# Splitting the near and the state products of a state space layer into runs, with the near products two blocks ahead

## The chip, the cores and the metric

The kernel runs on one core of a Trainium2 chip, as one program with one launch. The metric is the device time of one execution in microseconds (us), as the median over several executions. TensorE (PE) multiplies, VectorE (DVE), ScalarE (ACT) and GpSimd (POOL) do the rest, SyncE (SP) starts most of the transfers. PSUM, the memory that PE writes to, has 8 banks; a bank holds 512 numbers of 32 bits in each of 128 partitions.

## What is computed

A chain of layers on one sequence of 2048 rows with 128 channels: a mixture of experts, attention in a window, the experts again, a latent attention with its experts, **a state space layer**, and the latent attention with its experts once more. The change concerns the state space layer alone:

```python
def _L1_attn_ref(u, A_log, D, C_re, C_im, log_dt):
    dt = jnp.exp(log_dt)
    A = -jnp.exp(A_log)
    t = jnp.arange(L_, dtype=u.dtype)
    at = dt[:, None, None] * A[None, None, :] * t[None, :, None]
    K = jnp.einsum('mn,mln->ml', C_re, jnp.exp(at))
    u_f = jnp.fft.rfft(u.transpose(0, 2, 1), n=2 * L_)
    k_f = jnp.fft.rfft(K, n=2 * L_)
    y = jnp.fft.irfft(u_f * k_f, n=2 * L_)[..., :L_]
    return y.transpose(0, 2, 1) + u * D
...
x = x + _L1_attn_ref(_layernorm(x, axis=-1), ...)
```

Each channel is convolved with a kernel of its own that is a sum of 64 decaying exponentials, and gets its input times `D` and the residual added.

## The kernel before

Each layer is a stage. `leave_stage()` stands between stages: PE, DVE, ACT and POOL raise one semaphore when they are through, and all five engines wait for all four. So nothing of the following stage starts before the last instruction of the state space stage has ended.

`state_space` cuts the 2048 rows into `NT` = 16 tiles of 128 rows. For a channel m, what a tile gets from its own rows is a product with a 128x128 Toeplitz matrix (`toep[:, m, :]`); what it gets from all former tiles comes through 64 states. The steps:

1. `layer_norm` on DVE makes `Y`, tile by tile.
2. The states' inputs (L1999): 128 products, one for each channel, weights `b_in` 128x64, moving operand 16 columns of `Y`. They fill PSUM banks 0 and 1.
3. DVE copies these banks out (L2028), and one scan (L2030) runs the recurrence over the 16 tiles. `r_scanned` says that it is done.
4. DVE blanks banks 0 to 3 (L2032, four memsets), each raising `r_cleared`. The products write only 16 of every 32 partitions of a bank, and ACT reads all of them.
5. Eight blocks k of 16 channels each, block k in bank `k % 4`. A block has four groups (`qd`), and each group four **near** products (L2013: weights `Y[:, :, m]` 128x16, moving `toep` 128x128) and then four **far** or state products (L2020: weights the states 64x16, moving `E_far` 64x128), which add to the same places. The four of a group, q = 0 to 3, write partitions 32q to 32q+15: they lie in four column groups of PE's array. The far products take rows 0 to 63 or 64 to 127 of the array, by the parity of m.
6. After a block, ACT copies its bank into a row buffer in reversed order (L2045, raises `r_rows`), PE turns the four squares back (`turn_back`, L1992, into bank `4 + k % 2`, raises `r_turned`), and DVE adds the result to `X` (L2037, raises `r_added`).

PE's program is the plain order of the code: near and far of block k, `turn_back(k)`, near and far of block k+1. `turn_back(k)` waits for `r_rows` of its own block. POOL makes `Y * D` and adds it to `X` beside step 2 (`r_skip`).

The name `arena` in the profile is a large buffer that holds the inputs, the states and `toep`; `big_w` holds `E_far`; `ACCn` holds the row buffers; `Yn` is `Y`. In the stage before (latent attention) stands a line that the prediction uses, L1688: 16 products with weights 128x32 and a moving operand of 128x128, four after four into the four column groups, as near products do. L1618 uses the four column groups as well, L1592 and L1602 use half of the rows and all columns.

Of the kernel before, what the change touches and what calls it, by code (L numbers as in the profile page):

```python
# [12 lines left out]
P = 128  # L13
T = 2048
NT = T // P
# [33 lines left out]
def bcast(ap, n):  # L49
    return ap.unsqueeze(len(ap.shape)).broadcast_to(list(ap.shape) + [n])  # L50
# [27 lines left out]
def build(nc, ins, out, upto=6):  # L78
    with ExitStack() as ctx:
        pe, dve, act, pool, sp = nc.tensor, nc.vector, nc.scalar, nc.gpsimd, nc.sync  # L80
# [4 lines left out]
        def sem(name):  # L85
            return ctx.enter_context(nc.semaphore(name))


        psum = ctx.enter_context(nc.psum_tensor("psum", [P, 8, GW], F32))

        X, Yn, ACCn = sb("X", [P, NT, D]), sb("Yn", [P, NT, D + 1]), sb("ACCn", [P, NT, D + 1])
        Y, ACC = Yn[:, :, 0:D], ACCn[:, :, 0:D]
# [21 lines left out]
        def take(start, n, dt=F32):  # L114
            part = arena[:, start:start + n]
            return part if dt is F32 else part.bitcast(dt)
# [26 lines left out]
        toep = take(0, D * P).rearrange("p (m x) -> p m x", m=D)  # L143
# [23 lines left out]
        def chain(instruction):  # L167

            instruction.then_inc(dve_step.sem, dve_step.up())
            dve.wait_ge(dve_step.sem, dve_step.n)  # L170

        def leave_stage(pool_beside=None):

            for e in (pe, dve, act, pool):
                e.drain().then_inc(stage_left, 1)
            stages[0] += 1
            if pool_beside is not None:
                pool_beside()
            for e in (pe, dve, act, pool, sp):
                e.wait_ge(stage_left, 4 * stages[0])  # L180
# [29 lines left out]
        def own_pool(instruction):  # L210

            instruction.then_inc(pool_step.sem, pool_step.up())
            pool.wait_ge(pool_step.sem, pool_step.n)
# [55 lines left out]
        def layer_norm(n, x_ready):  # L269
            for g in range(NG + 1):  # L270
                if g:
                    ln_rows(n, g - 1)
                if g < NG:
                    x_ready(g)
                    ln_statistics(n, g)
                    ln_rooted(n, g)
# [459 lines left out]
        def windowed_attention(n, f, x_ready):  # L736
# [404 lines left out]
            for g in range(NG):  # L1141
# [19 lines left out]
        back_in, rates_in, pair_made, rates_made, far_made, far_scaled, taps_out, toep_in, neg_made, near_made, near_exp = (  # L1161
            sem(n) for n in ("back_in", "rates_in", "pair_made", "rates_made", "far_made", "far_scaled", "taps_out", "toep_in",
                             "neg_made", "near_made", "near_exp"))
# [726 lines left out]
        def latent_block(B, n, c, f, x_ready, far):  # L1890
# [76 lines left out]
        r_padded, r_decay, r_skip, r_states_in, r_scanned, r_cleared, r_made, r_rows, r_turned, r_added = (  # L1967
            sem(n) for n in ("r_padded", "r_decay", "r_skip", "r_states_in", "r_scanned", "r_cleared", "r_made", "r_rows", "r_turned", "r_added"))
        C17 = NT + 1

        def state_space(n, x_ready):
            state_in, states, mult = (take(k * K, 64 * C17) for k in (96, 101, 106))
            v3 = lambda t: t.rearrange("p (a c) -> p a c", a=64)
            ysb = [ACC[:, 4 * i:4 * i + 4, :] for i in range(4)]
            layer_norm(n, x_ready)

            def ssm_pool():
                pool.memset(v3(state_in)[:, :, 0:1], 0.0)
                pool.memset(v3(mult)[:, :, 0:1], 0.0).then_inc(r_padded, 1)
                pool.tensor_copy(v3(mult)[:, :, 1:C17], bcast(decay[:], NT)).then_inc(r_decay, 1)  # L1980
                pool.wait_ge(skip_in, 16)
                pool.wait_ge(ln_normed, NT * (n + 1))
                own_pool(pool.tensor_tensor(ACC[:, :, :], Y[:, :, :], skip_d.unsqueeze(1).broadcast_to([P, NT, D]), ALU.mult))
                pool.tensor_tensor(X[:, :, :], X[:, :, :], ACC[:, :, :], ALU.add).then_inc(r_skip, 1)

            def ssm_pe():
                def turn_back(k):
                    pe.wait_ge(r_rows, k + 1)
                    if k >= 2:
                        pe.wait_ge(r_added, k - 1)  # L1990
                    for qd in range(4):
                        mm = pe.transpose(psum[:, 4 + k % 2, qd * P:(qd + 1) * P], ysb[k % 4][:, qd, :], ident[:])  # L1992
                    mm.then_inc(r_turned, 1)

                pe.wait_ge(near_exp, D // STEP)
                pe.wait_ge(ln_normed, NT * (n + 1))
                for a in range(64):
                    for r in range(2):
                        mm = pe.matmul(psum[64 * r:64 * r + 64, a // 32, (a % 32) * NT:(a % 32 + 1) * NT],  # L1999
                                       b_in[:, 2 * a + r, :], Y[:, :, 2 * a + r], start=True, stop=True)  # L2000
                mm.then_inc(r_states_in, 1)
                pe.wait_ge(toep_in, 16 * 8)
                st3 = v3(states)
                for k in range(8):
                    b = k % 4
                    if k < 4:
                        pe.wait_ge(r_cleared, k + 1)
                    else:
                        pe.wait_ge(r_rows, k - 3)
                    for qd in range(4):  # L2010
                        for q in range(4):
                            m = 16 * k + 4 * qd + q
                            pe.matmul(psum[32 * q:32 * q + NT, b, qd * P:(qd + 1) * P], Y[:, :, m], toep[:, m, :], start=True, stop=False,  # L2013
                                      skip_group_check=True)
                        if qd == 0 and k == 0:
                            pe.wait_ge(r_scanned, 1)
                        for q in range(4):
                            m = 16 * k + 4 * qd + q
                            r = 64 * (m % 2)
                            mm = pe.matmul(psum[32 * q:32 * q + NT, b, qd * P:(qd + 1) * P], st3[r:r + 64, m // 2, 0:NT],  # L2020
                                           E_far[r:r + 64, m // 2, 0:P], start=False, stop=True, skip_group_check=True)
                    mm.then_inc(r_made, 1)
                    turn_back(k)

            def ssm_dve():
                dve.wait_ge(r_states_in, 1)
                dve.wait_ge(r_padded, 1)
                chain(dve.tensor_copy(v3(state_in)[:, :, 1:C17], psum[:, 0:2, :].rearrange("p b (a c) -> p (b a) c", c=NT)))  # L2028
                dve.wait_ge(r_decay, 1)
                dve.tensor_tensor_scan(states, mult, state_in, 0.0, ALU.mult, ALU.add).then_inc(r_scanned, 1)  # L2030
                for b in range(4):
                    dve.memset(psum[:, b, :], 0.0).then_inc(r_cleared, 1)  # L2032
                dve.wait_ge(r_skip, 1)
                for k in range(8):
                    dve.wait_ge(r_turned, k + 1)
                    dst = X[:, :, 16 * k:16 * k + 16]
                    dve.tensor_tensor(dst, psum[:, 4 + k % 2, :].rearrange("p (m c) -> p c m", c=32)[:, 0:NT, :], dst, ALU.add).then_inc(r_added, 1)  # L2037

            def ssm_act():
                act.wait_ge(r_skip, 1)  # L2040
                for k in range(8):
                    act.wait_ge(r_made, k + 1)
                    if k >= 4:
                        act.wait_ge(r_turned, k - 3)
                    act.activation(ysb[k % 4], psum[:, k % 4, :].rearrange("p (k x) -> p k x", k=4)[:, :, ::-1], ACT.Copy).then_inc(r_rows, 1)  # L2045

            ssm_pool()
            ssm_pe()
            ssm_dve()
            ssm_act()  # L2050
            leave_stage()
# [84 lines left out]
```

## Time and profile before

| | |
|---|---|
| median of 3 runs | 1747.12 us (1745.82 to 1751.17) |
| the profiled execution | 1757.22 us |
| its span | 1755.9 us |
| mean granted clock of TensorE | 0.834 of 2.4 GHz |
| busy: PE, DVE, ACT, POOL | 1238.1, 1196.7, 947.0, 570.0 us |
| first product of the state space stage to its last add | 1075.17 to 1130.47 us |

A time in a row is counted from the start of the span. "Idle before" an instruction is time in which its engine did nothing, and the name behind the arrow is what ended it. An f32 product stands in the trace as two records on PE (a transpose as one). The granted clock is 1.00 at 2.4 GHz and 0.50 at 1.2 GHz; the chip grants it by what PE did before. The last chain of waits, which ends with the store, says nothing of this stage: it is read from the stretch between its two barriers.

### The profile page before, as it was taken

Reading aid. Unit: us, or ns where it says so; the run is one execution under the profiler, and the core shown is the slowest. Engines: PE = TensorE matmul, PEld = TensorE weight load, DVE = VectorE, ACT = ScalarE, POOL = GpSimd, SP = SyncE. Lnnn points to the kernel's source line nnn. Section 1 sums busy time; section 2 is a strip of 40 time slices with the busy share of each in tenths; the row PEclk is TensorE's granted clock in tenths of the full one; section 3 lists DMA queues with packets and bytes.
Section 4 is the critical chain, followed back from the end, with each engine's and each line's share of the span. In section 5 each row is a group of like instructions: output and inputs, shape, how many; then the busy total and the mean of one; then the engine's idle time right before and its main releaser. Section 6 shows DMA issues by size and latency. Waiting matters only on the chain. (4 is left out here: it accounts for less than half of the span.)

```text
span 1755.9 us, 36353 instructions
## 1 busy us (share of the span) xinstructions
PE 1238.1 (71%) x13313; PEld 624.7 (36%) x13313; DVE 1196.7 (68%) x3279; ACT 947.0 (54%) x1500; POOL 570.0 (32%) x1032
## 2 busy tenths in 40 slices
PE   2754564366757788899886464776778898988746
PEld 2653453365532122222232453353222222223246
DVE  4358598436777899987862354277789999786234
ACT  0226774122445688888875240134557788887522
POOL 2331276146662411321123242275332111112323
PEclk9977675577577999999998695856799999999869
DMA  9410000021001100000000180000000000000012
GB/s 243 102 46 1 1 4 2 22 66 50 1 18 53 35 1 1 1 2 3 1 1 13 49 217 27 2 1 1 1 1 2 1 2 1 1 2 1 13 44 81
DMA packets 59137, 49.01 MB, mean 28 GB/s; under 512 B 7105, under 2 KB 54194, under 8 KB 58610
## 3 DMA queue, kind: packets, MB, share of 16 engines
q1 hardware_dynamic: 53282, 35.84, 7.9%
q0 software_dynamic: 4736, 9.74, 1.7%
q8 instruction: 109, 1.79, 0.4%
q10 hardware_dynamic: 944, 1.10, 0.2%
q14 instruction: 66, 0.54, 0.1%
HBM read 32.72 MB, written 18.38 MB: 29 GB/s over the span
## 5 line engine op out<-in xcount | busy, mean ns | idle before, releaser
L1709 ACT ACTIVATE arena<-psum 128x1024 f32<-128x1024 f32 (+3 forms) x640 | 561.0, 898 | 191.6 <-PE psum L1602 170.8
L1761 DVE TENSOR_REDUCE arena<-psum 128x1 f32<-128x512 f32 x768 | 479.8, 683 | 63.4 <-PE psum L1592 59.7
L1618 PE MATMUL psum<-arena 128*9 128x256 f32 (+2 forms) x4352 | 346.4, 394 | 0.9 <-POOL arena L1826 0.4
L1592 PE MATMUL psum<-arena 64*128 64x512 bf16 (+3 forms) x1280 | 240.2, 371 | 128.7 <-DVE arena L1761 58.3
L1766 DVE CUSTOM_DVE_ANT_0 arena<-psum,wqkv 128x384 bf16<-128x384 f32 (+3 forms) x512 | 230.3, 486 | 89.0 <-PE psum L1592 75.1
L1602 PE MATMUL psum<-arena 64*128 64x512 bf16 (+3 forms) x1280 | 233.7, 362 | 20.0 <-ACT arena L1709 15.0
L1826 POOL TENSOR_SCALAR_AFFINE_SELECT arena<-arena 128x256 f32<-128x256 f32 x256 | 103.6, 408 | 323.0 <-ACT arena L1709 320.4
L1592 PEld LDWEIGHTS psum<-arena 64*128 64x128 bf16 x1280 | 64.0, 94 | 383.2 <-DVE arena L1761 196.6
L1618 PEld LDWEIGHTS psum<-arena 128*9 128x9 f32 x4352 | 67.7, 89 | 174.3 <-issue 133.5
L1804 POOL CAST arena<-arena 128x16 bf16<-128x16 f32 x64 | 16.4, 257 | 327.7 <-DVE arena L1772 325.4
L677 DVE TENSOR_SCALAR small<-psum,YT 128x128 f32<-128x128 f32 x168 | 50.5, 342 | 78.0 <-PE psum L587 77.4
L632 ACT ACTIVATE small<-psum,YT 128x128 f32<-128x128 f32 x168 | 52.4, 364 | 83.5 <-PE psum L587 64.6
L587 PE MATMUL psum<-arena,YT 128*128 128x128 f32 x672 | 97.1, 292 | 0.1
L1602 PEld LDWEIGHTS psum<-arena 64*128 64x128 bf16 x1280 | 63.5, 95 | 93.1 <-ACT arena L1709 46.6
L1714 ACT ACTIVATE arena<-psum 128x1024 bf16<-128x1024 bf16 x64 | 65.5, 1023 | 52.3 <-PE psum L1580 48.3
L587 PEld LDWEIGHTS psum<-arena,YT 128*128 128x128 f32 x672 | 87.6, 204 | 2.9 <-issue 1.3
L578 PE MATMUL psum<-ident,ACCn 128*128 128x128 f32 x16 | 7.2, 470 | 90.7 <-DMA ACCn<-sorted_rows 58.1
L559 POOL DMA_INDIRECT made_rows<-arena,index x38 | 42.4, 1116 | 76.8 <-DVE arena L657 75.1
L545 POOL DMA_INDIRECT sorted_rows<-Yn,slot x32 | 31.4, 980 | 83.9 <-DVE slot L363 74.8
L597 PE MATMUL psum<-w,small 128*128 x304 | 43.0, 286 | 15.7 <-ACT small L632 12.7
L1580 PE MATMUL psum<-identb,arena 128*128 128x128 bf16 x512 | 44.5, 237 | 9.9 <-DVE psum L1750 3.9
L597 PE MATMUL psum<-big_w,small 128*128 x368 | 50.5, 281 | 0.6 <-issue 0.6
(353 smaller groups left out, 1962.9 us busy)
## 6 DMA issues: line engine op xcount, KB each, us to landing
arena<-taps SPq DMA_DIRECT2D x8, 1024.0 KB
big_w<-in_w SPq DMA_DIRECT2D x2, 2048.0 KB
ACCn<-made_rows SPq DMA_DIRECT2D x16, 256.0 KB, 3.6
regions<-sorted_rows SPq DMA_DIRECT2D x5, 741.8 KB, 4.6
sorted_rows<-arena SPq DMA_DIRECT2D x2, 1483.5 KB, 16.8
ACCn<-regions SPq DMA_DIRECT2D x32, 64.5 KB, 1.9
w<-in_w SPq DMA_DIRECT2D x2, 1024.0 KB
ACCn<-sorted_rows SPq DMA_DIRECT2D x6, 258.0 KB, 3.4
```

What stands on the lines that cost most here:

```text
L587: mm = pe.matmul(hidden_of(s, k), first[s % 2][:, k * P:(k + 1) * P], xt[s // GT % 2][:, (s % GT) * P:(s % GT + 1) * P], start=True, stop= ...
L597: mm = pe.matmul(psum[:, 4 + s % 2, 0:D], hid[s % 2][:, k, :], flat2[:, bass.ds(expert[s] * HID + k * P, D)], start=(k == 0), stop=(k == H ...
L632: half = act.activation(hid[s % 2][:, k, :], hidden_of(s, k), ACT.Relu, bias=first[s % 2][:, HID + k:HID + k + 1])
L677: half = dve.tensor_scalar(hid[s % 2][:, k, :], hidden_of(s, k), first[s % 2][:, HID + k:HID + k + 1], 0.0, ALU.add, ALU.max)
L1592: pe.matmul(psum[:, b, 0:w], plain_q[v % 2][rows, a, i * P:(i + 1) * P], keys[rows, 2 * hq + a, c * GW:c * GW + w], start=True, stop=True) ...
L1602: mm = pe.matmul(psum[:, b + r, off:GW], keys[rows, 2 * hq + a, t * P:(t + 1) * P], shift_q[v % 2][rows, a, off:GW], start=True, stop=True)
L1618: mm = pe.matmul(psum[32 * hh:32 * hh + 9, O_BANK, lo:hi], values[:, tile_of(v, j), 4 * hq + hh, :], prob[(t + hh // 2) % N_PROB][:, hh % ...
L1709: act.activation(prob[t % N_PROB][:, :, off:GW], both, ACT.Exp, scale=INV_SQRT_HD).then_inc(a_got, 1)
L1714: act.activation(dst, bank.bitcast(BF16).rearrange("p (a t) -> p a t", a=2), ACT.Copy).then_inc(a_got, 1)
L1761: dve.tensor_reduce(place, bank[:, 0:w], AX.X, ALU.max).then_inc(a_max_got, 1)
L1766: dve.tensor_tensor_reduce(out=masked[cuts % 2][:, 0:w], in0=bank[:, 0:w], in1=causal[:, GW - w:GW], scale=1.0, scalar=LEAST, op0=ALU.add, ...
L1826: pool.affine_select(out=part, in_=part, compare_op=ALU.is_ge, fill=0.0, base=0, pattern=[[0, 2], [1, P]], channel_multiplier=-1).then_inc ...
```

## The change

Three edits, all in `state_space`:

- The states' inputs go to banks 6 and 7 instead of 0 and 1, and DVE reads them there. The four memsets of banks 0 to 3 stand first in `ssm_dve`, ahead of the wait for the states' inputs.
- A block is no longer four times (four near, four far) but 16 near (`near(k)`) and 16 far (`far_away(k)`). Only the first group of a block starts its bank (`start=(qd == 0)`).
- PE's order is near(0), near(1), the wait for the scan, and then for each k: far(k), near(k+2), turn_back(k-1); turn_back(7) comes last.

```diff
-                        mm = pe.matmul(psum[64 * r:64 * r + 64, a // 32, (a % 32) * NT:(a % 32 + 1) * NT],
+                        mm = pe.matmul(psum[64 * r:64 * r + 64, 6 + a // 32, (a % 32) * NT:(a % 32 + 1) * NT],
...
-                for k in range(8):
-                    b = k % 4
+
+                def near(k):
+
                     if k < 4:
                         pe.wait_ge(r_cleared, k + 1)
                     else:
...
-                            pe.matmul(psum[32 * q:32 * q + NT, b, qd * P:(qd + 1) * P], Y[:, :, m], toep[:, m, :], start=True, stop=False,
-                                      skip_group_check=True)
-                        if qd == 0 and k == 0:
-                            pe.wait_ge(r_scanned, 1)
+                            pe.matmul(psum[32 * q:32 * q + NT, k % 4, qd * P:(qd + 1) * P], Y[:, :, m], toep[:, m, :], start=(qd == 0),
+                                      stop=False, skip_group_check=True)
+
+                def far_away(k):
+
+                    for qd in range(4):
...
                     mm.then_inc(r_made, 1)
-                    turn_back(k)
+
+                pe.wait_ge(toep_in, 16 * 8)
+                near(0)
+                near(1)
+                pe.wait_ge(r_scanned, 1)
+                for k in range(8):
+                    far_away(k)
+                    if k + 2 < 8:
+                        near(k + 2)
+                    if k:
+                        turn_back(k - 1)
+                turn_back(7)
 
             def ssm_dve():
+                for b in range(4):
+                    dve.memset(psum[:, b, :], 0.0).then_inc(r_cleared, 1)
                 dve.wait_ge(r_states_in, 1)
...
-                for b in range(4):
-                    dve.memset(psum[:, b, :], 0.0).then_inc(r_cleared, 1)
```

PE's instructions from the states' inputs to the first `turn_back`, before (L1999 the states' inputs, L2013 near, L2020 far, L1992 `turn_back`):

```order
L1999 MATMUL psum<-Yn,arena 64x16 x128
L2013 MATMUL psum<-arena,Yn 16x128 x4
L2020 MATMUL psum<-big_w,arena 16x128 x4
L2013 MATMUL psum<-arena,Yn 16x128 x4
L2020 MATMUL psum<-big_w,arena 16x128 x4
L2013 MATMUL psum<-arena,Yn 16x128 x4
L2020 MATMUL psum<-big_w,arena 16x128 x4
L2013 MATMUL psum<-arena,Yn 16x128 x4
L2020 MATMUL psum<-big_w,arena 16x128 x4
L1992 MATMUL psum<-ident,ACCn 128x128 x4
```

The same place now (the far products are L2022), down to the second `turn_back`:

```order
L1999 MATMUL psum<-Yn,arena 64x16 x128
L2013 MATMUL psum<-arena,Yn 16x128 x32
L2022 MATMUL psum<-big_w,arena 16x128 x16
L2013 MATMUL psum<-arena,Yn 16x128 x16
L2022 MATMUL psum<-big_w,arena 16x128 x16
L2013 MATMUL psum<-arena,Yn 16x128 x16
L1992 MATMUL psum<-ident,ACCn 128x128 x4
L2022 MATMUL psum<-big_w,arena 16x128 x16
L2013 MATMUL psum<-arena,Yn 16x128 x16
L1992 MATMUL psum<-ident,ACCn 128x128 x4
```

Where PE changed between near and far seven times in a block, it now changes once, two blocks' near products stand ahead of the first far one, and each `turn_back` has 32 products of other blocks between itself and the far products of its own block.

DVE's instructions in the stage, before (-) and now (+), from the end of the layer norm on:

```order
 L266 TENSOR_SCALAR Yn<-X,meanvar,rstd 128x128 x4
-L2028 COPY arena<-psum 128x64x16
-L2030 SCALAR_TENSOR_TENSOR arena<-arena 128x1088
-L2032 MEMSET psum 128x512 x4
-L2037 TENSOR_TENSOR X<-psum,X 128x16x16 x8
+L2040 MEMSET psum 128x512 x4
+L2043 COPY arena<-psum 128x64x16
+L2045 SCALAR_TENSOR_TENSOR arena<-arena 128x1088
+L2050 TENSOR_TENSOR X<-psum,X 128x16x16 x8
```

The four memsets moved from behind the scan to ahead of the copy; the number of instructions is the same on every engine.

## Rows read from the trace of the kernel before

**Rows 1.** The page's head.
```profile
span 1755.9 us, 36353 instructions
```

**Rows 2.** Windows: the stage in parts; stretch, length, busy (instructions), clock, DMA, GB/s.
```profile
1075.10:1089.05 13.95, 13.84 (x256) 13.76 (x256) 0.01 (x1) 0.00 (x0) 8.35 (x2) 0.50 0.01 2
1089.05:1093.40 4.35, 0.00 (x0) 0.00 (x0) 4.16 (x4) 0.00 (x0) 0.00 (x0) 0.50 0.00 0
1093.40:1102.30 8.90, 8.05 (x108) 2.74 (x108) 1.85 (x4) 0.60 (x1) 0.00 (x0) 0.50 0.01 2
1102.30:1130.55 28.25, 22.70 (x444) 10.24 (x436) 2.97 (x7) 4.18 (x7) 0.00 (x0) 1.00 0.01 2
1130.55:1755.90 625.35, 482.90 (x4469) 197.18 (x4469) 458.83 (x1278) 375.68 (x526) 191.30 (x431) 0.86 0.04 11
```

**Rows 3.** Waits from 1065 to 1145: total us, times, longest.
```profile
PE psum L1992 <- ACT ACCn L2045: 5.8, 8, 0.8
PE psum L2013 <- DVE psum L2032: 4.5, 1, 4.5
```

**Rows 4.** Timeline: states' inputs to first far products; start, length, engine, line, idle before.
```profile
1075.17 13.84 PE L1999 MATMUL psum<-Yn,arena 128*64 128x16 f32 x256 [23.08 <-DVE Yn L266]
...
1089.05 1.22 DVE L2028 COPY arena<-psum 128x1024 f32<-128x1024 f32 x1 [14.02 <-PE psum L1999]
1090.30 2.42 DVE L2030 TENSOR_TENSOR_SCAN arena<-arena 128x1088 f32<-128x1088 f32 x1
1092.83 2.11 DVE L2032 MEMSET psum<- 128x512 f32 x4
...
1093.46 0.63 PE L2013 MATMUL psum<-arena,Yn 128*16 128x128 f32 x8 [4.46 <-DVE psum L2032]
...
1094.03 0.62 PE L2020 MATMUL psum<-big_w,arena 64*16 64x128 f32 x8
```

**Rows 5.** Timeline: block 3, at the full clock.
```profile
1108.57 0.66 PE L1992 MATMUL psum<-ident,ACCn 128*128 128x128 f32 x4 [0.72 <-ACT ACCn L2045]
...
1109.16 0.43 PE L2013 MATMUL psum<-arena,Yn 128*16 128x128 f32 x8
...
1109.52 0.41 PE L2020 MATMUL psum<-big_w,arena 64*16 64x128 f32 x8
...
1111.60 0.41 PE L2020 MATMUL psum<-big_w,arena 64*16 64x128 f32 x8
1112.08 0.60 ACT L2045 ACTIVATE ACCn<-psum 128x512 f32<-128x512 f32 x1 [3.56 <-PE psum L2020]
...
1112.73 0.66 PE L1992 MATMUL psum<-ident,ACCn 128*128 128x128 f32 x4 [0.72 <-ACT ACCn L2045]
...
1113.42 0.42 DVE L2037 TENSOR_TENSOR X<-psum,X 128x256 f32<-128x256 f32 x1 [3.73 <-PE psum L1992]
```

**Rows 6.** Timeline of PE: two runs of L1688 at the full clock.
```profile
791.71 1.08 PE L1688 MATMUL psum<-big_w,pairs 128*32 128x128 f32 x32
792.73 0.28 PE L1602 MATMUL psum<-arena 64*128 64x256 bf16 x2
...
804.37 1.08 PE L1688 MATMUL psum<-big_w,pairs 128*32 128x128 f32 x32
805.24 0.64 PE L1618 MATMUL psum<-arena 128*9 128x256 f32 x8
```

**Rows 7.** Windows: two stretches at whose end the clock rose.
```profile
1221.80:1225.30 3.50, 3.04 (x18) 0.52 (x18) 2.51 (x9) 2.94 (x5) 2.17 (x7) 0.50 0.01 2
251.20:259.30 8.10, 5.88 (x208) 5.26 (x208) 7.89 (x12) 5.39 (x15) 5.77 (x5) 0.58 0.01 2
```

**Rows 8.** Timeline: the stage's end and the following stage's first products.
```profile
1129.36 0.66 PE L1992 MATMUL psum<-ident,ACCn 128*128 128x128 f32 x4 [0.72 <-ACT ACCn L2045]
1130.05 0.42 DVE L2037 TENSOR_TENSOR X<-psum,X 128x256 f32<-128x256 f32 x1 [3.73 <-PE psum L1992]
...
1133.97 0.66 PE L1249 MATMUL psum<-ident,ACCn 128*128 128x128 f32 x2 [3.95 <-DVE ACCn L1455]
```

More of the change, by code:

```diff
@@ L1998, in ssm_pe @@
                     for r in range(2):
-                        mm = pe.matmul(psum[64 * r:64 * r + 64, a // 32, (a % 32) * NT:(a % 32 + 1) * NT],
+                        mm = pe.matmul(psum[64 * r:64 * r + 64, 6 + a // 32, (a % 32) * NT:(a % 32 + 1) * NT],
                                        b_in[:, 2 * a + r, :], Y[:, :, 2 * a + r], start=True, stop=True)
                 mm.then_inc(r_states_in, 1)
-                pe.wait_ge(toep_in, 16 * 8)
                 st3 = v3(states)
-                for k in range(8):
-                    b = k % 4
+                def near(k):
                     if k < 4:
@@ L2019, in ssm_pe @@
                             r = 64 * (m % 2)
-                            mm = pe.matmul(psum[32 * q:32 * q + NT, b, qd * P:(qd + 1) * P], st3[r:r + 64, m // 2, 0:NT],
+                            mm = pe.matmul(psum[32 * q:32 * q + NT, k % 4, qd * P:(qd + 1) * P], st3[r:r + 64, m // 2, 0:NT],
                                            E_far[r:r + 64, m // 2, 0:P], start=False, stop=True, skip_group_check=True)
                     mm.then_inc(r_made, 1)
-                    turn_back(k)
+                pe.wait_ge(toep_in, 16 * 8)
[9 more added lines that the diff above has]
+                turn_back(7)
             def ssm_dve():
+                for b in range(4):
+                    dve.memset(psum[:, b, :], 0.0).then_inc(r_cleared, 1)
                 dve.wait_ge(r_states_in, 1)
                 dve.wait_ge(r_padded, 1)
-                chain(dve.tensor_copy(v3(state_in)[:, :, 1:C17], psum[:, 0:2, :].rearrange("p b (a c) -> p (b a) c", c=NT)))
+                chain(dve.tensor_copy(v3(state_in)[:, :, 1:C17], psum[:, 6:8, :].rearrange("p b (a c) -> p (b a) c", c=NT)))
                 dve.wait_ge(r_decay, 1)
                 dve.tensor_tensor_scan(states, mult, state_in, 0.0, ALU.mult, ALU.add).then_inc(r_scanned, 1)
-                for b in range(4):
-                    dve.memset(psum[:, b, :], 0.0).then_inc(r_cleared, 1)
                 dve.wait_ge(r_skip, 1)
```

## The prediction

> **What bounds the kernel now.** I read the windows first. The state space stage lies between two barriers, so its length from the first product at 1075.17 to the last add at 1130.05 + 0.42 = 1130.47 goes in full into the span of 1755.9 us [rows 1, 4, 8]. The windows show five parts [rows 2]: 13.95 us of states' inputs with PE busy throughout and DVE idle; 4.35 us in which PE does nothing and DVE 4.16; 8.90 us of products at half the clock; 28.25 us at the full clock with PE busy for 22.70; and the rest of the kernel. ACT and DVE are busy for a small part of the last two, so PE's order and PE's waits set the stage. No transfer runs in it that matters (DMA share 0.00 to 0.01), so the taps of `toep` are in.
>
> The waits show what PE stands for [rows 3]: eight times for ACT's copy before a `turn_back`, 5.8 us together, and once 4.5 us for the first memset. The timeline shows the chain behind the latter [rows 4]: copy, scan, memset, product.
>
> One block in the steady part [rows 5] runs from the start of one `turn_back` to the next: 1108.57 to 1112.73, 4.16 us. That is 0.59 of transposes (to 1109.16), a near group to 1109.52 (0.36), far and near groups in turn until the last far group starts at 1111.60 and ends at 1112.01, and 0.72 of waiting for ACT. So a near and a far group take (1111.60 - 1109.52) / 3 = 0.69 us, and the near one 0.36 of it.
>
> **The blanking.** The four memsets (2.11 us) move beside the states' inputs, where DVE waits 14.02 us [rows 4]. They end by 1077.3, before any product needs them, and the products no longer wait for one. The inputs go to other banks, which costs nothing. Before, the first near product started at 1093.46, 0.74 after the scan's end at 1090.30 + 2.42 = 1092.72 [rows 4]; now PE waits for the scan alone. I take 0.08 from a wait's end to the product (the ACT copy of block 3 ends at 1112.68, its transpose starts at 1112.73 [rows 5]), so the first far product starts at 1092.80.
>
> **The near products ahead of the scan.** near(0) and near(1) are eight groups. At half the clock a group takes 1094.03 - 1093.46 = 0.57 us [rows 4]; if a long run takes no less they need 4.5 us and end at about 1093.5, else about 3.5 us (below) and end at 1092.4, hidden under copy and scan. What hides them is 3.7 us of DVE's chain; without that cover they would cost their own length.
>
> **Runs of 16.** The trace has a run just like near(k): L1688, 16 f32 products of 128x32 by 128x128 in the four column groups. Its first record starts at 804.37, and L1618, which uses the array in the same four groups, follows at 805.24: 0.87 us. The other run starts at 791.71, and L1602, which uses half the rows and all columns, follows at 792.73: 1.02 us [rows 6]. Four near groups of today take 4 x 0.36 = 1.44. So what follows the same cut of the array starts 0.15 us earlier than what follows another cut, and a group that changes the cut at each end pays (0.36 - 0.87/4) = 0.14 for it. At half the clock 0.57 - 0.15 leaves 0.42, twice 0.21: the 0.15 does not grow with the slower clock. The Trainium skill ("TensorEngine Tiling (Array Packing)", Key Properties) says that changing the tiling mode, not just the tile, drains TensorE; near products are 128 rows by 32 columns, far ones 64 by 32, so by that rule the change removes drains, and by its absence the sum would be that of the first rival. The trace agrees, 0.87 against 1.02.
>
> Now near(k) takes 0.87 + 0.15 = 1.02, and a far run the same less what its groups are shorter by (0.69 - 0.36 = 0.33 against 0.36 a group): 4 x 0.33 - 3 x 0.15 = 0.87 at the least, 1.02 at the most; I take 1.00. The two bounds differ by 1.2 us over eight blocks.
>
> **The turns.** turn_back(k-1) stands behind far(k) and near(k+2), 2.0 us after its own far products, and ACT needs 0.07 + 0.60 + 0.05 = 0.72 [rows 5]. The wait goes in seven blocks. Other waits added: near(k+2) waits from k = 2 on for ACT's copy of block k-2, ended a block earlier; ACT and DVE work on the same data as before in blocks of 2.6 us, with 0.60 and 0.42 each. None becomes late. The wait of turn_back(7) stays: from the start of far(7), its 1.08 [rows 6] and 0.72.
>
> **The sum, at the full clock, from 1092.80.** Block 0: far 1.00, near 1.02. Blocks 1 to 5: 1.00 + 1.02 + 0.59 = 2.61 each, 13.05. Block 6: far and one turn, 1.59. Block 7: 1.08 + 0.72 = 1.80 (turn_back(6), 0.59, fits in it). Together 18.46, so turn_back(7) starts at 1111.26 where it started at 1129.36 [rows 8]: 18.1 us less. Behind it everything stands as before.
>
> **The clock.** Before, PE idled 4.46 us behind the states' inputs, began near products at half the clock and got the full one at 1102.3, 8.9 us later [rows 2, 4]. The states' inputs themselves, 13.84 us of busy PE, were given half the clock throughout. In other stretches the clock rose 3.5 us after products began again, or 8.1 us [rows 7]. Now products run from 1088.95 with one gap of about 0.4. By these rows the rise comes between 1092.4 and 1097.0; I take 1094.8, which leaves 2.0 us at half the clock behind 1092.80. A pair of runs at half the clock is 2 x (2 x 0.87 + 0.15) = 3.8 us against 2.02, so each such us gives (3.8 - 2.02) / 3.8 = 0.47 us late, 0.9 in all. Ends of this term: 0, and 4.2 if 8.9 us of low clock follow the scan. It also rests on these products being denser than those of today.
>
> **Forecast.** 18.1 - 0.9 = 17.2 us less. The profiled execution would come from 1757.2 to 1740.0; it lies 10.1 above the median of the runs, which would come from 1747.1 to 1729.9. Its own range, with the far runs and the clock at either end and 2 us of scatter, is 1726.5 to 1734.5.
>
> **Rivals.**
> 1. *A run gives nothing; only the waits go.* If each group keeps its 0.36 and 0.33 in a run too (because the four column groups' next weights can't come early, say), near(0) and near(1) end at 1093.5, and from there: block 0 2.8, blocks 1 to 5 5 x (2.76 + 0.59) = 16.8, block 6 1.91, block 7 1.40 + 0.72 = 2.12; 23.6, so the last turn starts at 1117.1, plus 0.5 for the clock. Less 11.8: 1735.3. For it: no row shows a far run of 64 rows by 32 columns in f32. Against it: the runs of L1688.
> 2. *The clock stays low longer.* With the turns between the runs as in the forecast but the rise only 8.9 us behind the scan: 18.1 - 4.2 = 13.9 less, 1733.2. For it: 13.84 us of states' inputs did not raise the clock. Against it: the rise at 1102.3 came through a stretch that was idle or in transposes for part of the time. The Trainium skill ("TensorE: Matmul & The Clock Gate", Part 4) says that transposes don't count as busy for the clock; they would then be 0.59 of each 2.61 instead of each 4.16 us and speak for this rival, and by it the time is that of this paragraph. The trace at the full clock from 1102.3 on, through seven turns [rows 2], shows that they don't lower it at 4.16 us a block.
> 3. *The edits cancel.* If the turns of other blocks, put between products, and the ACT waits behind them cost what they free, the stage stays near 55 us: 1747. Against it: ACT's 0.72 has 2.0 us of cover.
> 4. *Slower, by the clock of the following stage.* Its 625.35 us have a mean clock of 0.86 [rows 2], so some 175 us at half. PE is busy for 482.90 of it. If starting it 17 us earlier, after a denser stage, gave it more time at half the clock, each such us would cost up to 0.47; it needs 17.2 / 0.47 = 37 us more to eat the gain and 48 us for a time of 1752. For it: nothing but that the clock changes often there. Against it: PE idles from 1130.02 to 1133.97 in front of it [rows 8] as it will then, and the three runs lie within 5.4 us.
>
> **How the numbers follow.** Forecast 0.70, rival 1 0.13, rival 2 0.11, rival 3 0.03, rival 4 0.03. The range of 1726.5 to 1736 holds the forecast's range and the first two rivals. A measurement tells some 0.3%, 5 us, from no change; faster by more than that holds the first three cases, 0.94; the same 0.04; slower 0.02.
>
> **What would show it.** PE's idle time before the first product falls from 4.46 us to nothing, with one of about 0.4 before the first far run; near and far runs of 16 start 1.0 us apart at the full clock; `turn_back` waits for ACT once, for about 0.2 us; the copy waits as long as before, and the memsets lie at 1075 to 1077; the stage's last add ends at about 1113. Runs of 1.3 us and more would show rival 1, a clock of 0.50 beyond 1097 rival 2. An idle PE between far(k) and near(k+2) would show a wait that I have called early.

## The result

| | before | changed |
|---|---|---|
| median of 4 runs | 1747.39 us (1745.82 to 1751.17) | 1728.82 us (1726.56 to 1731.27) |
| profiled execution, span | 1757.22, 1755.9 us | 1726.56, 1725.3 us |
| state space stage, first product to last add | 55.30 us | 37.18 us |

The ratio is 0.9891, with a 95% interval of 0.9869 to 0.9913: 18.6 us less. Timed again on another occasion, five runs against nine of the kernel before, it was 1736.01 against 1756.98, ratio 0.9889 (0.9868 to 0.9910), 21.0 us less by the medians. The forecast was 17.2 less, to 1729.9.

The two first profiles differ by 30.6 us in span, 18.1 of it in the stage. The rest lies where nothing was changed: the stage starts 4.4 us earlier, and what follows it takes 617.4 us in place of 625.4. This isn't the change: a second profile of each kernel has spans of 1755.1 and 1738.3 and stages of 53.77 and 37.10, 16.8 us between the spans and 16.7 between the stages, and there 625.2 us follow the changed stage. Such differences go in part with the chip or the occasion: four of the variants below were profiled on one chip and have 617.5 to 619.1 us behind the stage, the other seven profiles come from two other chips and have 621.6 to 626.6. Why is open. So I compare stages below, not spans.

### The profile page after: what moved, and what is told of

Same layout as the page of the kernel before. It is cut to its first block and busy times, and to the rows that moved or that the text cites. A ratio compares the mean times of both kernels' runs of the same rounds, so it can differ in the third digit from the quotient of the medians.

```text
span 1725.3 us, 36353 instructions
## 1 busy us (share of the span) xinstructions
PE 1228.5 (71%) x13313; PEld 627.6 (36%) x13313; DVE 1195.7 (69%) x3279; ACT 946.8 (55%) x1500; POOL 568.1 (33%) x1032
## 5 line engine op out<-in xcount | busy, mean ns | idle before, releaser
L1804 POOL CAST arena<-arena 128x16 bf16<-128x16 f32 x64 | 16.3, 254 | 326.0 <-DVE arena L1772 323.8
```

## The profile after

Windows of the changed kernel's stage (columns as in [rows 2]):

```profile
1070.75:1084.60 13.85, 13.84 (x260) 13.81 (x264) 1.91 (x4) 0.00 (x0) 8.35 (x2) 0.50 0.01 2
1084.60:1088.35 3.75, 3.55 (x64) 2.50 (x64) 3.65 (x2) 0.00 (x0) 0.00 (x0) 0.50 0.02 4
1088.35:1107.95 19.60, 18.98 (x480) 14.55 (x480) 3.40 (x8) 4.79 (x8) 0.00 (x0) 0.99 0.01 3
1107.95:1725.30 617.35, 478.12 (x4469) 194.37 (x4469) 458.79 (x1278) 375.49 (x526) 190.91 (x431) 0.87 0.04 11
```

The part in which PE did nothing (4.35 us [rows 2]) now holds 3.55 us of products beside the same 3.65 us of copy and scan. What followed it, 8.90 + 28.25 us, has become 19.60, nearly all at the full clock.

All of PE's waits in the stage:

```profile
PE psum L1999 <- DVE Yn L266: 22.8, 1, 22.8
PE psum L2022 <- DVE arena L2045: 0.2, 1, 0.2
```

The first is the wait for the layer norm, ahead of the stage's products, as before. The 4.5 us for a memset is gone, and of the 5.8 us for ACT [rows 3] nothing is long enough to be listed; 0.2 us for the scan is left. The wait of turn_back(7), 0.2 us by the starts in the next rows, is too short for this list.

The timeline answers to [rows 4, 5, 8]; the far products are L2022, ACT's copy L2058, DVE's add L2050:

```profile
1070.72 2.10 DVE L2040 MEMSET psum<- 128x512 f32 x4
1070.76 13.84 PE L1999 MATMUL psum<-Yn,arena 128*64 128x16 f32 x256 [22.76 <-DVE Yn L266]
...
1084.53 3.62 PE L2013 MATMUL psum<-arena,Yn 128*16 128x128 f32 x64
1084.64 1.22 DVE L2043 COPY arena<-psum 128x1024 f32<-128x1024 f32 x1 [11.81 <-PE psum L1999]
1085.90 2.42 DVE L2045 TENSOR_TENSOR_SCAN arena<-arena 128x1088 f32<-128x1088 f32 x1
1088.38 1.18 PE L2022 MATMUL psum<-big_w,arena 64*16 64x128 f32 x32 [0.22 <-DVE arena L2045]
1089.48 1.08 PE L2013 MATMUL psum<-arena,Yn 128*16 128x128 f32 x32
...
1100.87 1.07 PE L2022 MATMUL psum<-big_w,arena 64*16 64x128 f32 x32
1100.98 0.42 DVE L2050 TENSOR_TENSOR X<-psum,X 128x256 f32<-128x256 f32 x1 [2.17 <-PE psum L1992]
1101.87 1.08 PE L2013 MATMUL psum<-arena,Yn 128*16 128x128 f32 x32
1102.00 0.60 ACT L2058 ACTIVATE ACCn<-psum 128x512 f32<-128x512 f32 x1 [2.00 <-PE psum L2022]
1102.88 0.66 PE L1992 MATMUL psum<-ident,ACCn 128*128 128x128 f32 x4
1103.47 1.07 PE L2022 MATMUL psum<-big_w,arena 64*16 64x128 f32 x32
...
1106.05 1.44 PE L1992 MATMUL psum<-ident,ACCn 128*128 128x128 f32 x8
...
1106.83 0.66 PE L1992 MATMUL psum<-ident,ACCn 128*128 128x128 f32 x4
...
1107.52 0.42 DVE L2050 TENSOR_TENSOR X<-psum,X 128x256 f32<-128x256 f32 x1 [0.36 <-PE psum L1992]
```

A step in the steady part runs from 1100.87 to 1103.47: 2.60 us, with a far run of 1.00, a near run of 1.01 and the transposes of 0.59, and no idle time before any of them. It was 4.16 [rows 5]. The last two turns stand together in the row at 1106.05; the second of them starts at 1106.83. The stage from its first product to the first far one takes 17.62 us; before, the scan ended 17.55 us after that product [rows 4].

## Experiments

Each is told by its stage length, from one profiled execution. The reference points are 55.30 and 53.77 us (the two profiles of the kernel before) and 37.18 and 37.10 (the changed one). The clock differs between them, so its rise is given where it matters.

### The kernel before again, for the clock

> The kernel before once more, for the spread of the clock's rise. If the rise comes at another time than 9.0 us behind the first near product, each us less at half the clock should make the stage some 0.35 us shorter than 55.30.

Measured: a stage of 53.77 us. Windows from the first near product on:

```profile
1094.90:1099.20 4.30, 4.21 (x64) 1.25 (x64) 1.45 (x3) 0.00 (x0) 0.00 (x0) 0.50 0.01 4
1099.20:1130.50 31.30, 24.99 (x488) 11.39 (x480) 3.40 (x8) 4.78 (x8) 0.00 (x0) 1.00 0.01 2
```

The clock rose 4.2 us behind the first near product where it had taken 9.0, with the same program. The stage was 1.54 us shorter for 4.8 us less at half the clock: 0.32 us for each, near the 0.35 expected. So of what separates a profile of the kernel before from one of the changed kernel, 1 to 3 us is the clock.

### The blanking alone

```diff
+ (states' inputs to banks 6 and 7; the four memsets first in ssm_dve)
```

> The kernel before with one part of the change: states' inputs in banks 6 and 7, the four memsets ahead of them. Stage length (first product to last add) was 55.30 us before and 37.18 with the whole change. My theory: the memset (0.74 us on the path) goes and the first near group (0.57 us) now runs under copy and scan; 1.2 to 1.3 us less, a stage of 54.0. Rival (the blanking is the gate for most of the gain, because PE idles 4.4 us there and loses the clock): over 4 us less, a stage under 51.

Measured: 52.57 us. The start of the products:

```profile
1088.28 0.63 PE L2013 MATMUL psum<-arena,Yn 128*16 128x128 f32 x8
1088.38 1.22 DVE L2030 COPY arena<-psum 128x1024 f32<-128x1024 f32 x1 [11.81 <-PE psum L1999]
1089.64 2.42 DVE L2032 TENSOR_TENSOR_SCAN arena<-arena 128x1088 f32<-128x1088 f32 x1
1092.12 0.63 PE L2020 MATMUL psum<-big_w,arena 64*16 64x128 f32 x8 [3.21 <-DVE arena L2032]
```

The first near group stands under the copy, and the first far group starts 17.62 us behind the stage's first product, where it stood at 18.86 before [rows 4]: 1.24 us, as expected. The stage lost 2.7 against one profile of before and 1.2 against the other; what goes beyond 1.24 is put down to the earlier rise of the clock, at 1095.9 (4.7 us less at half the clock beside the first, at 0.32 for each). The rival of over 4 us is out.

### Runs of 16 alone

```diff
                     for qd in range(4):
                         for q in range(4):
-                            ... toep[:, m, :], start=True, stop=False, ...
-                        if qd == 0 and k == 0:
-                            pe.wait_ge(r_scanned, 1)
+                            ... toep[:, m, :], start=(qd == 0), stop=False, ...
+                    if k == 0:
+                        pe.wait_ge(r_scanned, 1)
+                    for qd in range(4):
                         for q in range(4):
```

> The kernel before with one part of the change: a block is 16 near and then 16 far products, all else (memsets behind the scan, each turn behind its own block) as before. My theory (each change between near and far costs 0.14 us at either clock): a block goes from 4.16 to about 3.3 us, the stage from 55.3 to 48.5. Rival (the runs gain only because they stand ahead of time, beside other waits): a stage of 55.

Measured: 47.20 us. A block, at the full clock (far products L2021, ACT's copy L2046):

```profile
1102.94 0.66 PE L1992 MATMUL psum<-ident,ACCn 128*128 128x128 f32 x4 [0.71 <-ACT ACCn L2046]
1103.53 1.08 PE L2013 MATMUL psum<-arena,Yn 128*16 128x128 f32 x32
...
1104.55 1.07 PE L2021 MATMUL psum<-big_w,arena 64*16 64x128 f32 x32
1105.68 0.60 ACT L2046 ACTIVATE ACCn<-psum 128x512 f32<-128x512 f32 x1 [2.79 <-PE psum L2021]
1106.33 0.66 PE L1992 MATMUL psum<-ident,ACCn 128*128 128x128 f32 x4 [0.72 <-ACT ACCn L2046]
```

A block takes 3.39 us in place of 4.16, with the wait for ACT as it was: 0.77 us for six changes fewer, 0.13 for one. Eight blocks give 6.2 us of the 8.1; the rest is near what the clock accounts for, which rose 2.8 us behind the first near product and not 9.0 (6.2 us at 0.32 is 2.0). The runs gain without being ahead of time: the rival is out.

### The old order, with one cut of the array

```diff
-                            mm = pe.matmul(..., st3[r:r + 64, m // 2, 0:NT], E_far[r:r + 64, m // 2, 0:P], ...)
+                            mm = pe.matmul(..., st3[:, m // 2, 0:NT], E_far[:, m // 2, 0:P], ...)
```

> The kernel before, in its old order, but the far products take all 128 rows of the states and of E_far in place of the 64 of their channel (each channel also gets its partner's state products, so that part of the output is another). Near and far then cut the array in the same way, 128 rows by 32 columns. My theory (the 0.14 us is the price of another cut of the array): the gaps inside a block go although the order is the old one; a block goes from 4.16 to about 3.2 us, the stage from 55.3 to 47.5. Rival (the price is for returning to a column group with other operands, or for the order of groups of four): 55.3.

Measured: 46.23 us. Groups within a block:

```profile
1099.86 0.43 PE L2013 MATMUL psum<-arena,Yn 128*16 128x128 f32 x8
...
1100.11 0.40 PE L2020 MATMUL psum<-big_w,arena 128*16 128x128 f32 x8
1100.32 0.40 PE L2013 MATMUL psum<-arena,Yn 128*16 128x128 f32 x8
1100.54 0.40 PE L2020 MATMUL psum<-big_w,arena 128*16 128x128 f32 x8
```

Near and far groups follow each other at 0.22 us, in the old order of four and four, where they needed 0.33 to 0.36 [rows 5], and a block takes 3.26 us in place of 4.16. Taking twice the rows costs nothing, and the gap of 0.13 goes. So the gap belongs to the change between 128 and 64 rows, not to the order nor to the operands. Nor does it lie in the two row halves that far products take in turn: the far runs of 16 above take them in turn too, and have no such gap. The clock rose here as early as in the runs of 16 (2.7 us behind the first near product), so the two stages can be compared. This is the rule of the Trainium skill that the prediction cites ("TensorEngine Tiling (Array Packing)", Key Properties), and the runs agree with it.

### Near products two blocks ahead, but dealt out in groups of four

```diff
 for qd in range(4):
     (four far products of block k)
+    near_group(k + 2, qd)
-(the whole near(k + 2) behind them)
```

> The changed kernel, with far(k) and near(k+2) dealt out in turn, four far and four near, so that near products are still two blocks ahead and turns still one block late, but PE changes between near and far eight times in a block. My theory (cost of a change of the array's cut): 7 more changes of 0.11 to 0.14 us in each of six blocks, 4.4 to 6 us, a stage of 41.6 to 43 where it was 37.18. Rival (what counts is that no ACT wait is left): 37.2.

Measured: 41.75 us. A step:

```profile
1099.48 0.41 PE L2028 MATMUL psum<-big_w,arena 64*16 64x128 f32 x8
...
1099.82 0.43 PE L2013 MATMUL psum<-arena,Yn 128*16 128x128 f32 x8
1100.18 0.41 PE L2028 MATMUL psum<-big_w,arena 64*16 64x128 f32 x8
...
1102.28 0.66 PE L1992 MATMUL psum<-ident,ACCn 128*128 128x128 f32 x4
1102.86 0.41 PE L2028 MATMUL psum<-big_w,arena 64*16 64x128 f32 x8
```

No wait for ACT is left here either, and the step is 3.38 us in place of 2.60. Six such steps make up the 4.6 us that the stage is longer. The step has seven changes between near and far where the changed kernel's has one, so six more and not the seven of the expectation: 0.13 us each.

### The turn right behind the far products

```diff
 far_away(k)
+turn_back(k)
 if k + 2 < 8:
     near(k + 2)
-if k:
-    turn_back(k - 1)
```

> The changed kernel with turn_back(k) right behind far(k), ahead of near(k+2): runs of 16 and near products ahead stay, the wait for ACT comes back. My theory: seven blocks wait about 0.8 us more, and the turn that stood in the last wait stands by itself, 6.2 us more, a stage of 43.4. Rival (PE's queue goes on with the following weights, so that the wait costs less): under 41.

Measured: 43.29 us. One step:

```profile
1110.21 1.07 PE L2022 MATMUL psum<-big_w,arena 64*16 64x128 f32 x32
1111.34 0.60 ACT L2056 ACTIVATE ACCn<-psum 128x512 f32<-128x512 f32 x1 [2.78 <-PE psum L2022]
1111.99 0.66 PE L1992 MATMUL psum<-ident,ACCn 128*128 128x128 f32 x4 [0.71 <-ACT ACCn L2056]
1112.58 1.08 PE L2013 MATMUL psum<-arena,Yn 128*16 128x128 f32 x32
```

From the far run to its turn it takes 1.78 us, where the next run stood 1.00 behind the far one. The order of the turns is worth 6.1 us. The clock doesn't come into it, nor into the experiments before and after this one: in all three it rose within 0.4 us of the first far product, as in the changed kernel.

### The turn behind the near run of its own step

```diff
 far_away(k)
 if k + 2 < 8:
     near(k + 2)
-if k:
-    turn_back(k - 1)
+turn_back(k)
```

> The changed kernel with one edit: turn_back(k) stands behind near(k+2) of its own step, so blocks are not turned back one later. My theory (ACT's copy, 0.72 us from the last far product to the turn, is hidden by any run of near products, 1.02 us): blocks 0 to 5 as before, and only blocks 6 and 7, which have no near run behind them, wait; a stage of 38.6 us where the changed kernel has 37.2. Rival (each turn needs a block's distance): over 42.

Measured: 38.46 us. Where near runs end:

```profile
1109.31 1.07 PE L2022 MATMUL psum<-big_w,arena 64*16 64x128 f32 x32
...
1110.30 1.08 PE L2013 MATMUL psum<-arena,Yn 128*16 128x128 f32 x32
...
1111.32 0.66 PE L1992 MATMUL psum<-ident,ACCn 128*128 128x128 f32 x4
1111.90 1.07 PE L2022 MATMUL psum<-big_w,arena 64*16 64x128 f32 x32
...
1113.68 0.66 PE L1992 MATMUL psum<-ident,ACCn 128*128 128x128 f32 x4 [0.71 <-ACT ACCn L2056]
```

With a near run in between, the turn of block 5 waits for nothing; those of blocks 6 and 7 wait 0.71 each. So turning back one block later gains 1.3 us at the end of the stage and nothing in its middle: the near run alone covers ACT.

### Near products ahead of the states' inputs

The states' inputs were given half the clock in every profile in which they come first, ten of them. This version puts near(0) and near(1) ahead of them, to have the clock up before.

PE's order in it:

```python
pe.wait_ge(toep_in, 16 * 8)
near(0)
near(1)
# here the 128 states' inputs, which stood ahead of all this
near(2)
near(3)
pe.wait_ge(r_scanned, 1)
far_away(0)
for k in range(8):
    if k + 1 < 8:
        far_away(k + 1)
    if k + 4 < 8:
        near(k + 4)
    turn_back(k)
```

> A version meant to be faster: near(0) and near(1) stand ahead of the states' inputs, near(2) and near(3) beside the copy and the scan; then far(0), and for each k far(k+1), near(k+4), turn_back(k). Theory A: the near products raise the clock and it stays up through the states' inputs, whose weights then load faster; these take 7 to 9 us in place of 13.84, and with 1.7 us more idle before the scan's end the stage comes to 31.5 to 34 us where the changed kernel has 37.2. Theory B: the states' inputs are given half the clock again, or take 13.84 us at any clock; the stage is 1.5 to 3 us longer than 37.2.

> The version with near(0) and near(1) ahead of the states' inputs, timed. Its stage was 35.68 us against 37.18 of the changed kernel, of which 0.6 go to the later first product. Expected against the kernel before: 18 to 20 us less; against the changed kernel 1 us less, which the scatter of the runs will hide.

Measured: stages of 35.68 and 33.30 us. Windows of the first profile, near(0) and near(1), then the states' inputs in two parts:

```profile
1080.40:1084.05 3.65, 3.56 (x65) 2.95 (x65) 1.46 (x3) 0.00 (x0) 3.65 (x1) 0.50 0.02 4
1084.05:1087.50 3.45, 3.45 (x122) 3.45 (x120) 0.00 (x0) 0.00 (x0) 3.37 (x2) 0.99 0.00 0
1087.50:1095.05 7.55, 7.55 (x148) 7.51 (x150) 0.00 (x0) 0.00 (x0) 0.86 (x1) 0.50 0.02 4
```

And PE's timeline of the second:

```profile
1077.26 3.29 PE L2008 MATMUL psum<-arena,Yn 128*16 128x128 f32 x64 [23.50 <-DVE psum L2042]
1080.48 8.55 PE L2026 MATMUL psum<-Yn,arena 128*64 128x16 f32 x256
1088.97 3.62 PE L2008 MATMUL psum<-arena,Yn 128*16 128x128 f32 x64
```

The clock rose 3.6 and 2.8 us behind the first near product, and at the full clock the records of the inputs started 29 ns apart, at half the clock 53. (The windows count a record in each stretch that it touches, so their counts add up to more than 256.) But the clock fell again, 3.4 us into the inputs in one profile and 6.4 in the other, so they took 11.02 and 8.55 us where they had taken 13.84. The second profile has the times of theory A, but not its clock; the first fits neither theory. Timed, the version has a median of 1736.62 us over five runs (ratio to before 0.9889, 0.9871 to 0.9908), the changed kernel beside it 1736.01: no difference that can be told. Against the kernel before it is 20.4 us less by the medians, a little more than the 18 to 20 expected; against the changed kernel it is 0.6 us more, not 1 less. Of the 1.5 to 3.8 us that its stage is shorter, 0.6 go to the first product's wait for a memset, and the 0.9 to 3.2 us that are left are too little for such timings to tell; whether the version gains anything is not settled.

### Near products dealt among the states' inputs

```diff
 (the loop over the states' inputs, a = 0 to 63, two products each)
+    if a % 16 == 15 and a < 63:
+        near_group(2, a // 16)
```

The fourth group of near(2) and near(3) follow the inputs; all else is as in the version above.

> The version with near(0) and near(1) ahead of the states' inputs, and in addition a group of four near products of block 2 behind each 32 of the first 96 states' inputs. In the version without these the clock rose with the near products and fell again 3.4 us into the states' inputs, whose 256 records then went from some 30 ns apart to 53.7. Theory A (the states' inputs load PE too little to keep the clock, and denser products among them keep it): the clock stays at 1.00, the inputs and three groups take 9 to 10 us, a stage under 33.5 us. Theory B (three groups are too few): it falls again, the stage is 35.5 to 36.5, the cuts costing 6 x 0.14 us.

Measured: 39.52 us. Windows:

```profile
1080.10:1083.50 3.40, 3.40 (x109) 3.06 (x106) 0.00 (x0) 0.00 (x0) 3.32 (x2) 1.00 0.00 0
1083.50:1100.60 17.10, 15.58 (x286) 13.03 (x283) 3.65 (x2) 0.60 (x1) 1.05 (x1) 0.50 0.01 3
```

The clock fell 3.3 us into the inputs, as soon as in the first profile without the dealt groups and sooner than in the second, and stayed down for 17.1 us, into the far runs. Theory A is out in this one profile, and theory B was 3 us too short. Beside the first profile without the dealt groups the stage is 3.8 us longer: the three groups, which lay under copy and scan there, take 1.5 us among the inputs, the inputs themselves 0.8 more, and the first two far runs at half the clock 3.44 us in place of 1.87.

### The changed kernel again

> The changed kernel once more, timed beside it: 17 to 20 us less than the kernel before, a stage between 37.0 and 38.5 us, depending on when the clock rises.

Measured: 1736.01 us against 1756.98, which is 21.0 us less and 1 more than expected, and a stage of 37.10, as expected. Here the clock rose 3.9 us behind the first near product, 0.1 us into the first far run.

## Why the prediction was right, point by point

- **The blanking and the near products ahead.** Forecast: the first far product 0.08 us behind the scan's end. Measured 1088.38 - 1088.32 = 0.06. PE's idle time there was put at about 0.4 us and is 0.2. The copy waits 11.81 us and not as long as before (14.02), since the memsets' 2.10 us now lie in that wait.
- **Runs of 16.** Forecast 1.02 for a near run and 1.00 for a far one, from the two runs of L1688. Measured 1.01 and 1.00. The first rival stood on the far run, of which the kernel before has no row; it is out by the trace, and one cut of the array in the old order closes the same gap.
- **The turns.** Forecast: no wait in seven blocks. Measured: none in seven, and turn_back(7) starts 0.78 us behind turn_back(6), whose transposes take 0.59, so it waits the 0.2 us forecast. That the turns stand one block later matters only at the end of the stage. The distance was read too small, though: between far(k-1) and turn_back(k-1) there stand near(k+1), the turn before, far(k) and near(k+2), in the steady part 3.6 us and 48 products of other blocks, where the prediction says 2.0 us and the section on the change 32. It falls to 2.6 us for block 5 and 1.6 for block 6. All of it is more than ACT's 0.72, so nothing hangs on the slip; the third rival, a stage of 55 us, is out.
- **The sum.** 18.46 us from the first far product to the last turn. Measured 1106.83 - 1088.38 = 18.45.
- **The clock.** This is the term that was off: 0.9 us, from a rise 5.9 us behind the first near product, that is 2.0 into the far products. It came 4.1 us behind it, and 3.9 in the second profile, 0.3 and 0.1 us into the far runs, so it cost 0.1 or nothing. It explains the difference between 17.2 forecast and 18.1 measured in the stage. The lower end of the term (nothing lost) was the right one. The long-clock rival didn't come about: in both profiles the clock stayed at 1.00 from there to the end of the stage, some 19 us with 0.59 us of transposes in each 2.60. The prediction also leaned on the products being denser than before. The profiles fit that without showing it: the rise came 2.7 to 4.1 us behind the first near product in the ten profiles whose first near products stand in a run or share one cut of the array with the far ones, and 4.2, 7.6 and 9.0 us behind it in the three with the old order and two cuts. Three are few, and the lowest of them lies beside the ten.
- **No slower stage behind.** 617.4 and 625.2 us follow the stage now, 625.4 and 624.7 before: the fourth rival has nothing in the profiles.
- **The time.** Forecast 17.2 us less, measured 18.6, with an interval of 15.2 to 22.9. The time alone therefore leaves out the first two rivals (12 and 13.9 less) only narrowly; it is the trace that does it. How near the median came is in part luck, since the same forecast stands against 21.0 us on the other occasion, and the stage, which is what was worked out, is 18.1 or 16.7 us shorter by the profile of before that is taken. The profiled execution was to take 1740.0 us and took 1726.6: the 10.1 us by which the first profile lay above the median did not carry over. And the range of 1726.5 to 1734.5 is narrower than the ends that it names; they add up to about 1726 to 1735.4.

The gain by parts, the first, second and last from comparisons of their own, the third worked out from the length of a run: 6.2 us for the runs (eight blocks at 0.77), 6.1 for the turns, 2.7 for the two near runs that lie under copy and scan (two at 1.0) and the memset (0.7), and 2.8 for the clock against the first profile of before (8.7 us less of it at 0.32). Together 17.8 of 18.1. Against the second profile the clock gives 1.3, and the sum is 16.3 of 16.7.

## What to carry to other kernels

Products that cut TensorE's array in different ways should stand in runs: here each change cost 0.13 to 0.15 us at either clock, more than half of a group's own 0.22. (At half the clock a group in a run takes (3.62 - 0.63) / 7 = 0.43 us, from eight groups in a row and one alone, and groups that alternate follow at 0.56 to 0.57.) A wait of 0.7 us on another engine's copy is best covered by a run of products that need nothing from it; once one such run stands in between, more distance gains only at the end of the stage. And where a run of the same form exists elsewhere in the trace, its duration is a good forecast: it gave the near run to 0.01 us here.

## What the runs showed of the hardware

- A product over 128 rows followed another at the same pace as one over 64 (groups 0.22 us apart), and mixing the two heights cost 0.13 us a time. With the full height even the old order had a shorter stage than runs of 16 at two heights, 46.2 against 47.2 us; its output is another one, and no run here shows the full height with the right output.
- The states' inputs (128x64 weights, 16 columns moving) kept PE busy without a gap for 13.8 us, and the clock was at half throughout in each of the ten profiles where they come first. Where they began with the clock up or about to rise, it fell after 3.4 and 6.4 us of them. A busy share of 1.00 on PE went with either clock.
- The same program, the kernel before, saw the clock rise 4.2 us after its near products began in one execution and 9.0 in another; a forecast of a stage with such a rise has that width, here 1.5 us.
